# Cross-attention and feed-forward block on one core: one product for the scores, P transposed on TensorE, work moved between stages

## What is computed

```python
x = x + xattn(layernorm(x), ctx)          # x, ctx: 16 sequences of 128 tokens, 256 wide
    q, k, v = (a @ W.T + b).reshape(B, 16 heads, 128, 16)   # a plain reshape, no transpose
    attn = softmax(where(causal, q k^T / 4)); out = (attn @ v).reshape(B, 128, 256) @ Wp.T + bp
x = x + ffn(layernorm(x))                 # 256 -> 1024 -> gelu -> 256
    block_quant: inputs and weights in blocks of 32 share an exponent, 3 mantissa bits
```

## Time and profile before

| | us |
|---|---|
| median of 3 runs (lowest, highest) | 335.81 (334.59, 336.73) |
| the profiled execution | 337.91 |
| its span, first to last instruction | 336.1 |

### The profile page before, as it was taken

The page is one execution under the profiler, slowest core; times in us unless marked ns, Lnnn a source line. Parts: engine busy times, 40 slices in busy tenths (PEclk is TensorE's granted clock), DMA queues, the critical chain, the costliest instruction groups (busy, mean ns, idle before and its releaser), DMA issues.

```text
span 336.1 us, 7336 instructions
## 1 busy us (share of the span) xinstructions
PE 296.6 (88%) x2857; PEld 218.6 (65%) x2864; DVE 181.1 (54%) x398; ACT 142.3 (42%) x271; POOL 72.5 (22%) x70
## 2 busy tenths in 40 slices
PE   2939999989999999999999994999979798599963
PEld 2826776867777787777777772777757336267742
DVE  6402571394833643463283368145333589989980
ACT  2522252342345236145334521242343456379953
POOL 5000000000200020020020036000100243588883
PEclk9975995999999999999999999699969659789999
DMA  7786511422141141132114104010300200001111
GB/s 203 221 108 225 154 29 37 87 46 61 31 96 27 39 100 40 53 64 64 33 24 103 27 8 96 15 34 18 64 0 2 51 15 16 16 31 47 47 51 47
DMA packets 37664, 20.38 MB, mean 61 GB/s; under 512 B 12789, under 2 KB 37377, under 8 KB 37633
## 3 DMA queue, kind: packets, MB, share of 16 engines
q1 hardware_dynamic: 34992, 17.33, 22.2%
q10 hardware_dynamic: 2640, 2.62, 2.6%
HBM read 7.35 MB, written 2.10 MB: 28 GB/s over the span
## 4 chain that ended last, share of the span: by engine, by line
PE 77%; DVE 8%; DMA 4%; SPq 4%; issue 3%; ACT 3%; POOL 0%; POOLq 0%; DVEq 0%; ACTq 0%
PE s_banks L884 22%; PE bank L826 12%; PE t_banks L898 6%; PE bank L922 5%; PE s_banks L871 5%; PE t_banks L877 4%; PE bank L937 4%; PE bank L1055 3%; DVE xn L690 3%; PE s_banks L1030 2%; PE t_banks L1030 2%; DMA w_rows<-in_L_xattn_Wv 2%; PE bank L1045 1%; SPq L233 1%; PE t_banks L892 1%
## 5 line engine op out<-in xcount | busy, mean ns | idle before, releaser
L635 DVE TENSOR_REDUCE negm<-s_banks 128x4 bf16<-128x512 f32 x64 | 44.2, 691 | 117.1 <-PE s_banks L884 117.1
L364 ACT ACTIVATE prob<-t_banks 128x512 f32<-128x512 f32 x64 | 38.2, 597 | 117.7 <-PE t_banks L898 117.7
L892 PE MATMUL t_banks<-QS,KS 16*128 16x128 f32 x512 | 84.6, 460 | 0.0
L884 PE MATMUL s_banks<-KS,QS 16*128 16x128 f32 x512 | 84.6, 460 | 0.0
L884 PEld LDWEIGHTS s_banks<-KS,QS 16*128 16x128 f32 x512 | 66.0, 326 | 14.7 <-issue 14.7
L892 PEld LDWEIGHTS t_banks<-QS,KS 16*128 16x128 f32 x512 | 66.1, 326 | 0.2 <-issue 0.2
L494 POOL TENSOR_TENSOR rs<-ve,neg_half 128x2 f32<-128x2 f32 x8 | 5.6, 694 | 158.3 <-DVE ve L684 158.3
L871 PE MATMUL s_banks<-mask_q,ident_b 128*128 128x256 bf16 x128 | 26.4, 291 | 11.5 <-DVE negm L635 7.0
L536 POOL TENSOR_TENSOR hq<-hrn,h_mag 128x1024 bf16<-128x1024 f32 x16 | 30.7, 1919 | 19.9 <-DVE hrn L776 19.4
L826 PE MATMUL bank<-cT,wT 128*128 128x256 f32 x128 | 34.7, 407 | 0.0
L898 PE MATMUL t_banks<-ident_b,negm 128*128 128x128 bf16 x256 | 26.5, 228 | 0.0
(11 more groups left out here) (123 smaller groups left out, 451.4 us busy)
## 6 DMA issues: line engine op xcount, KB each, us to landing
oden<-oT SPq DMA_DIRECT2D x64, 64.0 KB, 2.3
KS<-full SPq DMA_DIRECT2D x32, 64.0 KB, 2.6
QS<-full SPq DMA_DIRECT2D x32, 64.0 KB, 2.5
VS<-full SPq DMA_DIRECT2D x64, 32.0 KB, 2.1
out<-full SPq DMA_DIRECT2D x16, 128.0 KB, 1.7
X<-in_x ACTq DMA_DIRECT2D x1, 1536.0 KB, 7.8
cbuf<-in_ctx SPq DMA_DIRECT2D x6, 256.0 KB, 2.8
fc_rows<-in_L_ffn_w_fc SPq DMA_DIRECT2D x1, 1024.0 KB, 6.2
```

What stands on the lines that cost most here:

```text
L364: nc.scalar.activation(prob[:, k % 4, :, :, :].rearrange("p u s t -> p u (s t)"), t_banks[:, :, 0:2 * P], ACT.Exp, scale=SCALE).then_inc(s ...
L635: V.tensor_reduce(negm[:, k % 2, :].rearrange("p (u s) -> p u s", u=2), s_banks[:, :, 0:2 * P].rearrange("p u (s t) -> p u s t", s=2), axi ...
L884: ins = T.matmul(s_banks[:, u, s * P:(s + 1) * P], QS[par][rows, head(b, m)], KS[par][rows, head(b, m)], start=False, stop=(s == 1))
L892: T.matmul(t_banks[:, u, s * P:(s + 1) * P], KS[t_par][rows, head(b, m)], QS[t_par][rows, head(b, m)], start=False, stop=False)
```

## The change

Scores are computed once. A pair has four quarters (`NW`) instead of eight slots. `scores` (L989 after) writes eight score matrices, queries on the partitions, into all four banks of `s_banks`. `maxes` works on two of the banks at a time as before; `exps` takes four exponentials of 128x128, each with its row maximum as ScalarE's bias, and the factor 1/4 is put on the queries' projection. `transpose_probs` transposes the P's on TensorE, four per call, into the single bank `t_bank`; VectorE copies them to `probT` (`copy_pt`). The tokens' order within a head is changed, so that the permutation matrix goes, and GpSimd copies the stacked queries head by head (`queries_apart`, into `QC`).

`normalise` moves from VectorE to GpSimd, as four operations, and with `project_out`, `residual` and `quantise` one pair later; pairs 6 and 7, and the rounding of pair 5, come among the tiles. The weights' exponents and roundings are spread over pairs 0 to 5 in eight parts (the tables `EXPONENTS_AT` and `ROUNDED_AT`: pair and quarter, part), GpSimd's `round_off` in eight over pairs 2 to 5. `V1` is doubled. The first two tiles' `ffn_up` stand ahead of the last two `attend`s, gelu's table is loaded ahead. At the start, forty small products on ones run before the first transposes, the order of the first projections differs, and three of the first queries' four DMAs are issued by ScalarE. The loops over the tiles are written out.

The diff, cut to the core:

```diff
-            def stack_rows(p, par):
-                for t, (to, arrived) in enumerate(((KS, sm["k_stacked"]), (QS, sm["q_stacked"]))):
-                    sp.wait_ge(sm["proj_copied"], 3 * p + t + 1)
-                    for g in range(NG):
+            def stack_rows(p, par, t):
+                to, arrived = ((KS, sm["k_stacked"]), (QS, sm["q_stacked"]))[t]
+                sp.wait_ge(sm["proj_copied"], 3 * p + t + 1)
+                for g in range(NG):
+                    if p or t == 0 or g == NG - 1:
                         sp.dma_start(to[par][32 * g:32 * g + HD, :], full[t][:, g * P:(g + 1) * P])\
...
             def step(i, par, first, last):
+                if not last:
+                    if not first:
+                        sp.wait_ge(sm["s_done"], NW * i)
+                    stack_rows(i + 1, 1 - par, 0)
                 if not first:
                     move_out(i - 1)
                 if not last:
                     if not first:
-                        sp.wait_ge(sm["st_done"], NSLOT * i)
-                    stack_rows(i + 1, 1 - par)
+                        sp.wait_ge(sm["q_apart"], i)
+                    stack_rows(i + 1, 1 - par, 1)
+                    if not first:
+                        sp.wait_ge(sm["v_done"], i)
                     stack_values(i + 1, 1 - par)
                 if i < NPAIR - 4:
                     load_ctx(i + 2, par)
...
+            for g in range(NG - 1):
+                act.dma_start(QS[0][32 * g:32 * g + HD, :], full[1][:, g * P:(g + 1) * P]).then_inc(sm["q_stacked"], 16)
...
-            def exps(i, k):
-                act.wait_ge(sm["st_done"], NSLOT * i + k + 1)
-                if k >= 4 or type(i) is not int or i:
-                    act.wait_ge(sm["av_done"], 4 * i + k // 2 - 1)
-                nc.scalar.activation(prob[:, k % 4, :, :, :].rearrange("p u s t -> p u (s t)"),
-                                     t_banks[:, :, 0:2 * P], ACT.Exp, scale=SCALE).then_inc(sm["exp_done"], 1)
+            def exps(k):
+                act.wait_ge(sm["max_done"], k + 1)
+                if k >= 4:
+                    act.wait_ge(sm["pt_done"], k - 3)
+                for u in range(2):
+                    for s in range(2):
+                        ins = nc.scalar.activation(prob[:, k % 4, u, s, :],
+                                                   s_banks[:, 2 * (k % 2) + u, s * P:(s + 1) * P],
+                                                   ACT.Exp, bias=negm[:, k % 4, u, s:s + 1])
+                ins.then_inc(sm["exp_done"], 1)
...
+            def queries_apart(p, par):
+                pool.wait_ge(sm["q_stacked"], 16 * NG * (p + 1))
+                if p > 1:
+                    pool.wait_ge(sm["s_done"], NW * (p - 1))
+                nc.gpsimd.tensor_copy(QC[par][:, :, :].rearrange("p n (j w) -> p n j w", j=NJ // KC),
+                                      QS[par][:, :].rearrange("p (j n w) -> p n j w", j=NJ // KC, n=2 * NM))\
+                    .then_inc(sm["q_apart"], 1)
...
+            def normalise(p):
+                pool.wait_ge(sm["rden_done"], p + 1)
+                nc.gpsimd.tensor_tensor(by_token(off1[:, :]), by_group[1], by_group[2], ALU.mult)\
+                    .then_inc(sm["newton"], 1)
+                nc.gpsimd.tensor_tensor(by_token(nout[:, :]), by_group[0], by_group[2], ALU.mult)\
+                    .then_inc(sm["newton"], 1)
+                pool.wait_ge(sm["newton"], 3 * p + 1)
+                nc.gpsimd.tensor_scalar(off2[:, :], off1[:, :], -1.0, 2.0, ALU.mult, ALU.add)\
+                    .then_inc(sm["newton"], 1)
+                pool.wait_ge(sm["newton"], 3 * p + 3)
+                if p:
+                    pool.wait_ge(sm["y_done"], p)
+                nc.gpsimd.tensor_tensor(onrm[:, :, :, :].rearrange("p c b t -> p (c b t)"), off2[:, :],
+                                        nout[:, :], ALU.mult).then_inc(sm["onrm_done"], 1)
...
+                if i > 1:
+                    normalise(i - 2)
+                if i > 2:
+                    power2(i - 3)
...
+                if 2 <= i < 6:
+                    round_off(2 * i - 3)
+                if not last:
+                    queries_apart(i + 1, 1 - par)
+                else:
+                    normalise(i - 1)
+                    power2(i - 2)
...
-            def maxes(i, k):
-                dve.wait_ge(sm["s_done"], NSLOT * i + k + 1)
-                if k >= 2 or type(i) is not int or i:
-                    dve.wait_ge(sm["st_done"], NSLOT * i + k - 1)
-                V.tensor_reduce(negm[:, k % 2, :].rearrange("p (u s) -> p u s", u=2),
-                                s_banks[:, :, 0:2 * P].rearrange("p u (s t) -> p u s t", s=2),
+            dve.wait_ge(sm["q_stacked"], 16 * NG)
+            V.tensor_copy(QC[0][:, :, :].rearrange("p n (j w) -> p n j w", j=NJ // KC),
+                          QS[0][:, :].rearrange("p (j n w) -> p n j w", j=NJ // KC, n=2 * NM)).then_inc(sm["q_apart"], 1)
+            def maxes(k):
+                dve.wait_ge(sm["s_done"], k // 2 + 1)
+                V.tensor_reduce(negm[:, k % 4, :, :],
+                                s_banks[:, 2 * (k % 2):2 * (k % 2) + 2, 0:2 * P].rearrange("p u (s t) -> p u s t", s=2),
                                 axis=AX.X, op=ALU.max, negate=True).then_inc(sm["max_done"], 1)
+            def copy_pt(k):
+                dve.wait_ge(sm["pt_done"], k + 1)
+                if k >= 4:
+                    dve.wait_ge(sm["av_done"], k // 2 - 1)
+                V.tensor_copy(probT[:, k % 4, :, :, :].rearrange("p u s t -> p (u s t)"), pt_bank(k)[:, :])\
+                    .then_inc(sm["pt_copied"], 1)
...
+            EXPONENTS_AT = {(0, 3): 0, (1, 0): 1, (1, 1): 2, (1, 3): 3, (2, 1): 4, (2, 3): 5, (3, 3): 6, (4, 3): 7}
+            ROUNDED_AT = {(1, 0): 0, (1, 1): 1, (1, 2): 2, (2, 1): 3, (2, 2): 4, (3, 1): 5, (4, 1): 6, (5, 1): 7}
...
+                k = 2 * NW * i
+                if i > 2:
+                    residual(i - 3)
+                maxes(k)
+                if not first:
+                    copy_pt(k - 2)
+                maxes(k + 1)
+                if not first:
+                    copy_pt(k - 1)
+                if i > 2:
+                    stats2(i - 3)
+                weights_at(i, 0)
...
+                if t == 2:
+                    residual(NPAIR - 2)
+                    stats2(NPAIR - 2)
+                if t == LAST_OUT + 1:
                     residual(NPAIR - 1)
...
+                if t == 0:
+                    quantise_rest(NPAIR - 3)
+                if t in (3, LAST_OUT + 2):
+                    quantise(NPAIR - 2 + t // LAST_OUT)
+                    quantise_rest(NPAIR - 2 + t // LAST_OUT)
...
+            for n in range(40):
+                ins = T.matmul(bank[3][:, 0:P], ones_b[:, :], ones_b[:, :], start=True, stop=True)
+            ins.then_inc(sm["warm"], 1)
...
-            def slot(i, k, par, s_on=True, t_on=True):
...
+            def scores(i, w, par):
+                if w == 0:
+                    pe.wait_ge(sm["k_stacked"], 16 * NG * (i + 1))
+                    pe.wait_ge(sm["q_apart"], i + 1)
+                if w or i:
+                    pe.wait_ge(sm["exp_done"], 2 * (NW * i + w))
+                for g in range(NG):
+                    T.matmul(s_banks[:, g, 0:2 * P], ident_b[:, :], mask_q[:, :, :].rearrange("p s t -> p (s t)"),
+                             start=True, stop=False)
                 for s in range(2):
...
+                    n = 2 * w + s
+                    for g in range(NG):
+                        rows = slice(32 * g, 32 * g + HD)
+                        ins = T.matmul(s_banks[:, g, s * P:(s + 1) * P], QC[par][rows, n, :],
+                                       KS[par][rows, :].rearrange("p (j n w) -> p n j w", j=NJ // KC,
+                                                                  n=2 * NM)[:, n],
+                                       start=False, stop=(s == 1))
+                ins.then_inc(sm["s_done"], 1)
+            def transpose_probs(k):
+                pe.wait_ge(sm["exp_done"], k + 1)
+                if k:
+                    pe.wait_ge(sm["pt_copied"], k if pt_bank(k) is t_bank else k - 1)
+                for u in range(2):
+                    for s in range(2):
+                        ins = T.transpose(pt_bank(k)[:, (2 * u + s) * P:(2 * u + s + 1) * P],
+                                          prob[:, k % 4, u, s, :], ident_f[:, :])
+                ins.then_inc(sm["pt_done"], 1)
...
-                values(i, par)
+                k = 2 * NW * i
+                scores(i, 0, par)
+                if not first:
+                    transpose_probs(k - 2)
+                    attend(i - 1, 2)
+                if not last:
+                    trans_x(i + 1)
+                if not first:
+                    transpose_probs(k - 1)
+                if last:
+                    trans_weights(0)
+                    trans_weights(1)
+                else:
```

(65 more changed lines are left out.)

555 lines of the change are left out of this document (280 added, 275 removed).

## The result

The kernel after takes 271.63 us (median of 4 runs, 271.03 to 272.67) against 335.82 (334.59 to 336.73) beside it on the same chip: ratio 0.8094 [0.8058, 0.813], 64 us less. The profiled execution took 271.03 us, its span is 269.2, and the mean granted clock is 0.962 (before 0.917).

What follows compares the result with a forecast made beforehand. TensorE was taken to bound attention, VectorE the feed-forward part. 22.5 + 2 + 8 x 23.5 = 212.5; last scores end 3.9 earlier, 208.6; + 7.5 + 65 + 9.8 = 290.9 of span, so 293 us, range 275 to 322.

Steps and rivals of the forecast that it cites:

- the price of the score products: TensorE's sixteen score weight loads and products per quarter, taken to stay at 1.27 us as in one old slot.
- the faster case: Rival: score products at 0.92 us save 1.4 us a pair, no stalls save 0.7; 276 us in all, chance 0.17.
- The lower end: Lowest price considered for a quarter's sixteen score instructions on TensorE: 0.92 us, from four that take 0.23.
- TensorE's order: TensorE's sequence through a pair's four quarters, with second transposes waiting for VectorE's copy of the first: 22.8 us a pair.
- the 0.7 us of stalls: Per pair, VectorE waiting on ports shared with GpSimd: 1.5 us, half absorbed, 0.7 added to reach 23.5.
- eight exponentials: ScalarE's 128-column exponentials in a quarter: 7 x 0.26 + 0.37 = 2.2 us, lying under the projection.
- Transposes: Eight added groups of four fp32 transposes of P per pair on TensorE: 0.44 us a group, 3.5 together.
- The late copy of the queries: GpSimd's copy into QC, ending near 21 us into a pair; next scores want it at 22.8, room under 2 us.
- the rival of handoffs: Rival: engine handoffs, slower exponentials and a late queries' copy make a pair 27 us, 321 in all; chance 0.25.
- The clock rival: Rival: TensorE's waits lose its full clock; at half the time low, a pair is 30.8 us, 351 whole; chance 0.08.
- The ends: Outside the pairs: first scores at 22.5 us, 2 for a slow first pair; after last scores 7.5, 65 and 9.8.

Runs made afterwards that it cites:

- the kernel with slow reads: The kernel after with both operands of the score products read eight elements apart again, as in the kernel before: 286.59 us, ratio 0.8567.
- the late loads: The kernel after with w_proj's load issued behind the second pair's stacked rows, 266.82 us; or w_fc's there and w_proj's a pair later, 267.85 us.

## Why the prediction was wrong, and where it was right

**The step that failed** is the price of the score products: "I take 1.27, the same operation's row." They took 0.65, at 1.00 of granted clock in both cases. That is 4 x 0.62 = 2.5 us a pair. Times eight it is 20, which nearly equals the 19.5 missed between the first and the last scores, but by luck: put back by experiment, the slow reads cost 15.0 us (286.59 for 271.63). The other 6.4 of the 21.4 us by which 293 was too high have other sources, and the kernel with slow reads shows where they lie: from its first to the end of its last scores it takes 181.5 us for a forecast 186.1, mostly since its first two pairs take 22.67 and 22.55 for 25.5 and 23.5, and the end is 1.5 shorter.

The row was that of an operation with the same name and shape but not with the same reads, and the row that could have decided stood beside it: at the lower clock the products took the same 1.27, while the projection beside them took 3.73 for 1.95. Something other than the array paced them. The forecast said so, named the spacing as one possible cause, looked only at the weights' side of it (the keys' reads changed as well), and gave it 0.17.

The Trainium skill has the rule (SBUF — State Buffer, Door 1: The DMA port swizzle): SBUF is read in lines of 16 bytes, an access that goes on to a new line pays, so a stride of up to four fp32 values is free. Eight apart is 32 bytes, past that. The trace agrees with the direction: 1.26 us against 0.65. It also agrees that the moving operand of after, in runs of 16 values, is as fast as a fully contiguous one (0.65 and 0.66). Weighed beside the earlier trace rows it was a reason to give the faster case more than 0.17.

**The lower end was wrong too.** 0.92 came from the four products that add the maxima, 0.23 us for bf16 products of 128x128. They are another operation with another shape: sixteen score products of 301 ns each come and go within 0.65 us, so they overlap, and how closely nothing in those four showed. With 0.92 the rival gave 276, and 271.6 lay outside even that.

**The kernel with slow reads is what was priced**, and it checks the rest of the sum: pairs of 23.26 for 23.5, 286.6 us for 293. TensorE's order is so 23.3 and not 22.8, and the 0.7 us of stalls that were added on top are not there; the two errors nearly cancel.

**ScalarE** was right: eight exponentials were forecast in 2.2 us, and in its timeline the row of one quarter has 2.34, the pieces 0.28 apart on average:

```profile
106.34 2.34 ACT L392 ACTIVATE prob<-s_banks,negm 128x128 f32<-128x128 f32 x8 [0.71 <-DVE negm L725]
```

**Transposes** were priced at 0.44 a group and take 0.43 to 0.59 from start to next start (107.13 to the next group at 107.56, 105.47 to 106.06).

**The late copy of the queries** was placed well. It was forecast to end 21 us into a pair, with room for under 2 us. The timeline of GpSimd in the pair that starts at 109.52, whose follower starts at 130.34:

```profile
127.18 1.05 POOL L607 TENSOR_TENSOR pj_q<-pj_rows,w_mag 128x512 bf16<-128x512 f32 x1
128.94 1.04 POOL L553 COPY QC<-QS 128x1024 f32<-128x1024 f32 x1 [0.71 <-DMA QS<-full]
```

and VectorE's beside it:

```profile
129.20 1.25 DVE L685 TENSOR_SCALAR xn<-X,mv,rs 128x256 f32<-128x256 f32 x2
```

The copy ends at 129.98, 20.5 us into the pair and 0.36 us before the scores that need it; in the other steady pairs it ends 0.9 to 1.2 us before them. It took 1.04 us, not the 1.9 to 3.65 of the bounds; at those it would have been late in this pair. So the rival of handoffs (321 us) was avoided in the steady pairs by a small margin; it did come once, at the second pair, by 5.1 us, from a cause that it did not name: landing times of 7 to 8 us under the weights' loads.

**Stalls by GpSimd.** Forecast 0.7 us a pair; found nothing on the path. VectorE's row above is of the kind that was feared: two operations of 128x256 take 1.25 beside the copy, and 0.73 elsewhere (108.37). A delay of 0.5 us, off the path. The longest GpSimd operation in a pair is 1.27 us, not 1.9. The rule of the Trainium skill on the shared ports (SBUF — State Buffer, Who interferes with whom) holds here as an upper bound: in the rows read, no such operation was longer by more than GpSimd's own beside it (the longest pair of them, at 212.58, took 1.37 beside one of 1.91). The stall of 7 us is gone, as forecast.

**The clock rival** (351 us) fell. The steady pairs have a granted clock of 1.00, though TensorE waits a few tenths of a microsecond in two quarters of four and transposes 32 score matrices a pair. The Trainium skill's rule that the full clock does not engage for transposes (TensorE: Matmul & The Clock Gate, Part 4: PE-mode transpose) is not borne out where at least 32 of a pair's 224 recorded products are transposes; a stretch of transposes alone is not in these runs.

**The ends.** The first tile's maxima come 8.6 us after the last scores, not 7.5 and before 8.7: placing the tiles ahead brought some 0.5 and not 1.2. The tiles took 64.1 for 65, and before 59.1; that the 5 us more are VectorE's work carried over from attention fits the forecast, but no run tests it. The end was 1.5 shorter than before.

## What to carry to other kernels

The price of a product holds only with its operands' spacing: before using a row for a changed kernel, compare the reads as well as the shape, and treat a product that takes the same time at either clock as one that the array doesn't pace. Put both operands side by side: one alone brought 0.10 or 0.14 of the 0.61 us here. When a change frees the bounding engine, look at the first stages too, where bulk loads share the queues with small DMAs that now come to be waited for.

## What was not expected of the hardware

fp32 products with 16 rows take 0.65 us for sixteen instructions with both operands nearly contiguous, 1.12 with the moving one eight apart, 1.16 with the weights so, 1.26 with both. The moving operand of after is not fully contiguous (runs of 16 values), and the kernel before with fully contiguous ones is no faster (0.66). At a granted clock of 0.50 the same sixteen take 1.17 with both nearly or fully contiguous and 1.27 with both eight apart, so there the spacing costs little.

Small copies from SBUF to SBUF of 64 KB land after 7 to 8 us (median) instead of 2.3 while loads of 1024 KB, issued by the same engine, are under way.

What stays open: why the kernel after varies by 6 us (266.04 to 272.52) on one chip, what its fastest executions do otherwise, and whether the gain of the late loads (3 to 5 us by medians, under 1 by the fastest runs) can be had in full.
